# A quad's shared rows fetched and turned first, its last two experts' rows later, and an earlier normalisation on ScalarE in the router stage

## What is computed

```python
x = x + 0.5 * L0_ffn(layernorm(x))          # quantised 256x256 weight plus a low-rank term
x = x + L0_attn(layernorm(x))               # 16 heads, sums over dyadic sets of keys
x = x + 0.5 * L0_ffn(layernorm(x))
x = x + 0.5 * L1_ffn(layernorm(x))          # router, 32 experts, 16 adapters
x = x + L1_attn(layernorm(x))               # linear attention
x = x + 0.5 * L1_ffn(layernorm(x))
...
# L1_ffn: the router takes each normalised row with five of its statistics
ri = concat([xf, stats(xf)]); h = gelu(ri @ r1_w.T + r1_b); probs = softmax(h @ r2_w.T)
topp, topi = top_k(probs, 2)
idx = argsort(-where(routed, probs, -inf), axis=0)[:cap].T     # cap = 160 rows of each expert
up = einsum('eci,eji->ecj', xf[idx], w_up); gate, upv = split(up)
ye = einsum('ecj,eoj->eco', silu(gate) * upv, w_down)
out = zeros.at[idx].add(w * ye)                                # plus the adapters' part
```

## Time and profile before

| | us |
|---|---|
| median of 3 runs | 1788.64 (1785.24 to 1790.99) |
| the profiled execution, device time | 1788.87 |
| its span | 1787.2 |
| TensorE matmul busy | 1488.8 (83% of the span) |
| VectorE busy | 977.1 (55%) |
| ScalarE busy | 728.9 (41%) |
| GpSimd (POOL) busy | 564.3 (32%) |
| mean granted TensorE clock | 0.908 of full speed |

### The profile page before, as it was taken

One profiled execution on the slowest core, in us unless ns is written; L12 is line 12 of the kernel. 1 busy time (PEld: TensorE's weight loads), 2 busy tenths in 40 slices (PEclk: granted clock), 3 DMA queues, 4 the chain that ended last, 5 costly groups with the idle time before them and its releaser, 6 DMA issues. The chain is left out here.

```text
span 1787.2 us, 27066 instructions
## 1 busy us (share of the span) xinstructions
PE 1488.8 (83%) x9512; PEld 1127.3 (63%) x9512; DVE 977.1 (55%) x2816; ACT 728.9 (41%) x1775; POOL 564.3 (32%) x467
## 2 busy tenths in 40 slices
PE   6899989999999678339999997489995459999994
PEld 5566544555554454229889997255553349899994
DVE  8865677787873597855531111356566855521110
ACT  5222147666667375415423232114333425322331
POOL 6522210000000442321636455221211231636535
PEclk9989889999999898559999999699997569999997
DMA  3034363333300022325969894401112326879974
GB/s 104 18 127 129 107 131 63 79 55 79 55 26 1 12 95 83 150 44 174 246 194 258 245 246 65 133 25 35 48 36 95 118 71 201 225 221 247 265 193 47
DMA packets 113493, 212.11 MB, mean 119 GB/s; under 512 B 20085, under 2 KB 79386, under 8 KB 104154
## 3 DMA queue, kind: packets, MB, share of 16 engines
q1 hardware_dynamic: 87066, 178.93, 31.8%
q0 software_dynamic: 26304, 31.60, 11.4%
HBM read 158.71 MB, written 51.38 MB: 118 GB/s over the span
## 5 line engine op out<-in xcount | busy, mean ns | idle before, releaser
L952 DVE TENSOR_REDUCE attnm_top<-psum 128x1 f32<-128x384 f32 (+3 forms) x384 | 212.8, 597 | 56.4 <-PE psum L1037 52.3
L1174 ACT ACTIVATE attnm_prob<-psum 128x512 f32<-128x512 f32 (+1 forms) x384 | 192.1, 530 | 87.6 <-PE psum L1047 81.0
L2328 POOL DMA_INDIRECT x_sum<-moe1e_y,moe_scatter_i x76 | 119.7, 1575 | 128.2 <-ACT moe1e_y L2462 71.0
L2507 DVE SCALAR_TENSOR_TENSOR moe1e_h<-moe1e_gate,psum 128x160 f32<-128x160 f32 x160 | 50.6, 321 | 199.4 <-ACT moe1e_gate L2436 199.1
L2328 POOL DMA_INDIRECT out<-moe2e_y,moe_scatter_i x76 | 119.2, 1568 | 127.7 <-ACT moe2e_y L2462 70.5
L2507 DVE SCALAR_TENSOR_TENSOR moe2e_h<-moe2e_gate,psum 128x160 f32<-128x160 f32 x160 | 50.4, 321 | 198.8 <-ACT moe2e_gate L2436 198.6
L2383 PE MATMUL psum<-moe1e_xgT,moe_w_up 128*128 128x160 f32 x1024 | 152.2, 304 | 2.4 <-ACT moe1e_xgT L2452 2.4
L2383 PE MATMUL psum<-moe2e_xgT,moe_w_up 128*128 128x160 f32 x1024 | 150.7, 302 | 2.4 <-ACT moe2e_xgT L2452 2.4
L2383 PEld LDWEIGHTS psum<-moe1e_xgT,moe_w_up 128*128 128x128 f32 x1024 | 144.2, 193 | 4.8 <-issue 4.8
L2383 PEld LDWEIGHTS psum<-moe2e_xgT,moe_w_up 128*128 128x128 f32 x1024 | 142.7, 192 | 4.8 <-issue 4.8
L1348 POOL DMA_INDIRECT moe_xg<-xn_rows,moe_gather_i x80 | 84.3, 1054 | 159.3 <-DVE moe_gather_i L1536 93.0
(11 more groups left out here) (414 smaller groups left out, 3230.5 us busy)
## 6 DMA issues: line engine op xcount, KB each, us to landing
moe_w_up<-in_expert_up SPq DMA_DIRECT2D x64, 1024.0 KB, 7.5
moe_w_down<-in_expert_down SPq DMA_DIRECT2D x64, 512.0 KB, 3.5
attnm_q_hat<-q_parts SPq DMA_DIRECT2D x72, 128.0 KB, 4.4
moe_a_up<-in_adapter_up SPq DMA_DIRECT2D x32, 256.0 KB, 4.2
q_parts<-attnf_q_part SPq DMA_DIRECT2D x12, 512.0 KB, 2.8
attnm_k_hat<-k_parts SPq DMA_DIRECT2D x72, 64.0 KB, 2.3
x_res<-in_x SPq DMA_DIRECT2D x8, 512.0 KB, 9.4
v_tails<-attnf_v_tail SPq DMA_DIRECT2D x4, 1024.0 KB, 4.3
```

The lines of the kernel that those rows point to most:

```text
L952: nc.vector.tensor_reduce(top[:, n // QUADS % 2, tiles[0]:tiles[-1] + 1, hh:hh + 1], s.ps[:, u.bank, 0:len(tiles) * width].rearrange("p (t ...
L1174: nc.scalar.activation(prob[:, i % NPROB, at:GROUP], s.ps[:, u.bank, at:GROUP], ACT.Exp).then_inc(taken[u.bank], 1)
L2328: nc.gpsimd.indirect_dma_start(total, bass.IndirectOffsetOnAxis(ap=rows, axis=0), y[:, q, k, :], None, bounds_check=TOKENS + SPARE - 1, oo ...
L2507: nc.vector.scalar_tensor_tensor(out=h[:, n % 2, i, :], in0=gate[:, i, :], scalar=1.0 if i < INTER // P else SCALE_A, in1=s.ps[:, u.bank, ...
```

## The change

A second table, `FETCHED`, replaces `TWO` for gathering and turning: tile 4 alone, then tiles 0 and 1, then 2 and 3. The batches of x become separate entries of `ORDER`. For the even quad of a turn, the batch of tiles 2 and 3 is turned and copied after `up` of the first expert, and `up` waits for it only at the third expert of the quad. The odd quad still turns its three batches together. `weights` follows the last batch. In `ffn_router`, `norm(i + 3)` moves from ahead of the gelu to right behind `copy(i + 2)`.

```diff
--- before.py
+++ after.py
@@ -1214,6 +1214,7 @@
 LOW = [4 ** k for k in range(7, -1, -1)]
 ROUNDS = len(HIGH) + len(LOW)
 TWO = [(0, 1), (2, 3), (4,)]
+FETCHED = [(4,), (0, 1), (2, 3)]
 ALONE = TWO[0]
 SIDE, HOTS = 4, 8
 
@@ -1342,7 +1343,7 @@
 
     def gather(self, pool, quad):
         q = quad % 2
-        for i, tiles in enumerate(TWO):
+        for i, tiles in enumerate(FETCHED):
             for k in tiles:
                 at = quad * ST_TILES + k
                 pool.indirect_dma_start(self.xg[:, q, k, :], None, self.rows,
@@ -2035,6 +2036,8 @@
                     r.take(act, i - 4)
                 if 0 <= i + 2 < GROUPS:
                     copy(i + 2)
+                if 0 <= i + 3 < GROUPS:
+                    norm(i + 3)
                 if 0 <= i - 1 < GROUPS:
                     r.absolute(act, i - 1)
                     r.under(act, i - 1)
@@ -2043,8 +2046,6 @@
                     r.copy_s(act, i - 2)
                 if 0 <= i - 1 < GROUPS:
                     r.copy_x(act, i - 1)
-                if 0 <= i + 3 < GROUPS:
-                    norm(i + 3)
                 if 0 <= i - 2 < GROUPS:
                     r.gelu(act, i - 2)
     st.close()
@@ -2223,9 +2224,9 @@
     ORDER = []
     for n in range(2 * EQ):
         if n == 0:
-            ORDER += [("x", 0, None)] + [("up", 0, i) for i in range(PAIRS)]
+            ORDER += [("x", 0, 0), ("x", 0, 1)] + [("up", 0, i) for i in range(PAIRS)] + [("x", 0, 2)]
         if n == 1:
-            ORDER += [("x", 1, None)]
+            ORDER += [("x", 1, j) for j in range(len(FETCHED))]
         if n + 1 < 2 * EQ:
             for i in range(PAIRS):
                 ORDER += [("up", n + 1, i)]
@@ -2243,9 +2244,8 @@
         elif what == "down":
             u_down[n] = banks.use(5)
         else:
-            for j in range(len(TWO)) if what == "x" else (i,):
-                (u_x if what == "x" else u_y)[n, j] = banks.use(6 + ring % 2)
-                ring += 1
+            (u_x if what == "x" else u_y)[n, i] = banks.use(6 + ring % 2)
+            ring += 1
 
     late = m.choices[1]
     STEPS = [("halves", None), ("counts", 0)]
@@ -2343,16 +2343,15 @@
             pool.wait_ge(y_out[q], 16 * (ST_TILES * 2 * TURNS - q * len(ALONE)))
 
     def tensor(pe):
-        def turn_x(t, q):
-            for i, tiles in enumerate(TWO):
-                u = u_x[q, i]
-                pe.wait_ge(x_in[q][i], 16 * len(tiles) * t + 16 * len(tiles))
-                pe.wait_ge(taken[u.bank], u.before(t))
-                for k, tile in enumerate(tiles):
-                    for c in range(CC):
-                        at = (c * len(tiles) + k) * P
-                        ins = nc.tensor.transpose(s.ps[:, u.bank, at:at + P], xg[:, q, tile, c * P:(c + 1) * P], s.ident[:])
-                ins.then_inc(full[u.bank], 1)
+        def turn_x(t, q, i):
+            u, tiles = u_x[q, i], FETCHED[i]
+            pe.wait_ge(x_in[q][i], 16 * len(tiles) * t + 16 * len(tiles))
+            pe.wait_ge(taken[u.bank], u.before(t))
+            for k, tile in enumerate(tiles):
+                for c in range(CC):
+                    at = (c * len(tiles) + k) * P
+                    ins = nc.tensor.transpose(s.ps[:, u.bank, at:at + P], xg[:, q, tile, c * P:(c + 1) * P], s.ident[:])
+            ins.then_inc(full[u.bank], 1)
 
         def turn_y(t, q, i):
             u, last = u_y[q, i], u_down[q * EQ + (TWO[i][-1] if i == 0 else EQ - 1)]
@@ -2369,8 +2368,8 @@
             if i == 0:
                 pe.wait_ge(up_in[k], 32 * t + 16 * q + 16)
                 pe.wait_ge(a_in[k // 2], 64 * t + 32 * q + 32)
-                if k == 0:
-                    for j in range(len(TWO)):
+                for j, tiles in enumerate(FETCHED):
+                    if k == tiles[0] % EQ:
                         pe.wait_ge(taken[u_x[q, j].bank], u_x[q, j].after(t))
             u = u_up[n, i]
             pe.wait_ge(taken[u.bank], u.before(t))
@@ -2414,7 +2413,7 @@
         def run(t, order):
             for what, n, i in order:
                 if what == "x":
-                    turn_x(t, n)
+                    turn_x(t, n, i)
                 elif what == "y":
                     turn_y(t, n, i)
                 elif what == "up":
@@ -2443,14 +2442,14 @@
             nc.scalar.copy(yT[:, q, :, k * P:(k + 1) * P], out_T[:, :, 0:P])
             nc.scalar.copy(yT[:, q, :, tail:tail + CAP - P], out_T[:, :, P:CAP]).then_inc(taken[u.bank], 1)
 
-        def copy_x(t, q):
-            for i, tiles in enumerate(TWO):
-                u, k = u_x[q, i], len(tiles)
-                act.wait_ge(full[u.bank], u.after(t))
-                slots = xgT[:, q].rearrange("p c (k n) -> p c k n", n=CAP)
-                slots = slots[:, :, tiles[0]:tiles[0] + k, 0:P] if tiles[0] < EQ else slots[:, :, :, P:CAP]
-                nc.scalar.copy(slots, s.ps[:, u.bank, 0:CC * k * P].rearrange(
-                    "p (c k n) -> p c k n", c=CC, n=P if tiles[0] < EQ else CAP - P)).then_inc(taken[u.bank], 1)
+        def copy_x(t, q, i):
+            u, tiles = u_x[q, i], FETCHED[i]
+            k = len(tiles)
+            act.wait_ge(full[u.bank], u.after(t))
+            slots = xgT[:, q].rearrange("p c (k n) -> p c k n", n=CAP)
+            slots = slots[:, :, tiles[0]:tiles[0] + k, 0:P] if tiles[0] < EQ else slots[:, :, :, P:CAP]
+            nc.scalar.copy(slots, s.ps[:, u.bank, 0:CC * k * P].rearrange(
+                "p (c k n) -> p c k n", c=CC, n=P if tiles[0] < EQ else CAP - P)).then_inc(taken[u.bank], 1)
 
         def weigh_y(t, q, i):
             u = u_y[q, i]
@@ -2478,7 +2477,7 @@
                 elif what == "down":
                     copy_down(t, n)
                 elif what == "x":
-                    copy_x(t, n)
+                    copy_x(t, n, i)
                 elif what == "y":
                     weigh_y(t, n, i)
                 else:
@@ -2532,7 +2531,7 @@
 
         def run(t, order):
             for what, n, i in order:
-                if what == "x":
+                if what == "x" and i == len(FETCHED) - 1:
                     weights(t, n)
                 elif what == "up":
                     product(t, n, i)
```

## The result

| | before | after |
|---|---|---|
| median of the runs, us | 1788.64 (1785.24 to 1791.51, 11 runs) | 1795.65 (1792.63 to 1800.18, 11 runs) |
| ratio to before | | 1.0039, 95% interval 1.0028 to 1.0050 |
| span of the profiled execution, us | 1787.2 | 1793.9 |
| router stage, first turn to first scores, us | 121.25 | 130.37 |
| first gather to `up`, first / second MoE, us | 10.81 / 10.36 | 8.30 / 8.17 |

The change costs 7.0 us (5.0 to 8.9 by the interval), where 0.4 us less than before was forecast. In its code the lines of the router front and of the MoE's front are one higher than before, those of the experts one lower (L1818, L1826, L1617 stand for L1817, L1825, L1616; L2382, L2353 for L2383, L2354).

A forecast was written before the change was run, and what follows sets the result against it. TensorE was taken to bound the experts' stretch and a loop through several engines the router stage. From 1788.87 us, -4.4 (experts' start), 0 (turn boundaries) and +3.7 (router stage) gave 1788.2 us, range 1783.5 to 1792.6.

The forecast's parts named there:

- the first term: Start of the experts in both MoEs: `up` waits for three gathers instead of five, together -4.4 us.
- The start of the experts, -4.4: `up` starts 2.36 us earlier in the first MoE and 2.01 in the second; bounds -6.2 to -2.5.
- The turn boundaries, 0 with 0.6 to each side: Later quads of each MoE: small gains at even quads and losses at odd ones cancel, 0 us.
- The router stage without the clock, +0.83: Router loop: early group 4 wins 2.08 us, two rounds of 12.72 us lose 2.91; net +0.83 at group 7's turn.
- the rival of the early turn kept: Router stage: TensorE's 5.84 us wait vanishes whole and rounds stay at 10.65 us; 1778.7 us, chance 0.10.
- the one of VectorE: Router stage: VectorE sets the pace, and its normalisations, freed from POOL's bias, save 8.2 us; 1776.3 us, chance 0.04.
- The clock, +2.9 for two of three losses at 1.45: Router stage: longer waits before hidden of groups 0 to 2 drop TensorE's clock, 1.45 us per loss; with +0.83, +3.7.
- The first pause: TensorE's wait before hidden of group 0, one of three taken to grow from 0.96 to 3.03 us.
- the clock stays low: Router stage: the lost clock stays at 1.2 GHz through logits and turn, 3.25 us per round; 1795.1 us, chance 0.07.

The follow-up runs named there:

- x only: The kernel before with only the new order of gathers and expert rows, norm at its old place; 1784.86 us, ratio 0.999.
- Norm only: The kernel before with only norm moved behind the copy, gathers unchanged; 1796.07 us, ratio 1.0047.
- filled kernel: The change plus transposes that nothing reads in TensorE's pauses ahead of group 0's statistics and hidden 1 and 2, router stage alone; 1783.88 us, ratio 0.9968.
- absolute values thrice: The kernel before with two more unused absolute values on ScalarE for each of groups 1, 2 and 3 in the router stage; 1800.38 us, ratio 1.0074.
- boundary filler: The kernel before with the new gather and row order, plus six unread transposes ahead of tile 4's turn and six ahead of `up` at each even quad; 1778.85 us, 0.9955.

## Why the prediction was wrong

The forecast was 1788.2 us and no difference that can be told; measured were 1795.65 us and 7.0 us more. In the profiles the first term came out at -4.7 us where -4.4 was forecast, and the router stage at +9.1 where +3.7 was. The two MoE stages behind their starts add 5.9 us (-0.4 and +1.0 of it in the first passes), where nothing was forecast, and stages that the change does not touch took 3.6 us less.

**The start of the experts, -4.4: right in place, too good in sum.** Both starts gained what the sum gave (2.51 and 2.19 us against 2.36 and 2.01), and from a gather's issue to its first transpose 3.38 to 3.67 us passed, not the 2.3 us worked out from the Trainium skill's page DMA: Bandwidth & Descriptors, section on the anatomy of one DMA. Alone the part measured -1.8 us by the ratio, with an interval from -4.5 to +0.7. The profile of x only loses 1.6 us again behind the second start, of which 1.0 are first passes at the lower clock. A loss of that kind lay in the bounds given.

**The turn boundaries, 0 with 0.6 to each side: the bound was wrong.** The waits and transposes came as worked out. That a boundary can lose the clock was not in the sum. In the change's profile it cost 0.5 us in one MoE and 3.9 in the other, in two other kernels 4.4 and 4.5 us in one MoE. The term should have had an upper end of some 4.5 us for a MoE. Whether the new order brings these losses is not shown. Norm only, in the old order, loses 8.4 us with none in its profile, so they are not the main part of the 7.0.

**The router stage without the clock, +0.83: right.** The filled kernel is the test. From turn 2 to hidden 0 it won 2.07 us (forecast 2.08). From turn 5 to turn 7 it lost 2.35 us (forecast 2.91), for a round of 12.45 instead of 12.72 us. Net that is +0.28 us. The loop copy, norm, absolute, under, count, hidden, turn is the mechanism, and the rival of the early turn kept falls with it, as does the one of VectorE: its normalisations all fell to 1.38 us, and the stage did not get shorter.

**The clock, +2.9 for two of three losses at 1.45: the step that failed.** The place and the cause were right, the size was not. Against the filled kernel the change lost 1.05 us between turn 2 and hidden 0, 0.48 up to turn 5 and 4.64 up to turn 7: 6.2 us for the term that was put at 2.9, with 5.3 as its upper end. Norm only lost the same 6.2 us (1.16, 1.56 and 3.46), divided otherwise. Three things went wrong in the price.

All three pauses lost the clock in norm only, at 1.52 to 1.58 us each in hidden alone. The first pause was misread: TensorE waited 0.29 us ahead of hidden 0, not 0.96, and what grows is the wait ahead of the statistics, to 3.91 us behind the early turn of group 4. The clock lost there delayed hidden 0 by 1 us more. And the slow stretch can outlast hidden. That cost the change 3.66 us in the round of its second loss (16.11 instead of 12.45) and 0.98 in the next, not 1.45. It lost the clock at two pauses of three, as the sum had it, but by luck: behind the long round TensorE waits only 1.04 us ahead of hidden 2, which no step of the forecast held.

The outlasting stretch was the rival "the clock stays low" (1795.1 us, chance 0.07), against which I put that "hidden alone gives TensorE work to bring the clock back". In norm only it did, in the change it did not at group 1: the clock stood at 0.50 from 654.10 to 667.00, while TensorE was busy 12.82 of 12.90 us. That the rival's 1795.1 us is close to the result is luck: of the three pauses one had its long loss in this profile, and the sum was made up by the first pause, hidden of group 6 and the boundaries.

The remaining 2.7 of the stage's 9.1 us lie where the change edits nothing, 1.13 ahead of turn 2 and 1.54 behind turn 7. They are the clock too, but not behind the new pauses, and norm only shows little of either with the same code there (11.00 and 59.51 us).

**Chances.** The upper ends of the terms together gave 1793.1 us, and the result lies above that as well as above the range. I cut the range to 1792.6 and gave 0.07 to slower, although the term with the widest bounds was priced from one row of a pause of 2.93 us that lost the clock for certain. That evidence pointed to three losses of three.

## What to carry to other kernels

Work moved ahead in an engine's order is free only if no loop between engines runs through the new place: here 2 us of ScalarE work made two rounds 2.4 us longer together (12.45 and 12.43 us against 11.88 and 10.65), and that was the smaller part. Price every TensorE pause that grows to 3 us with the work behind it at the lower clock, for each of them, and let the range reach to a slow stretch that outlasts the first matmuls. And before a pause is shortened by reordering, try filling it with work that nothing reads: it recovered 6.2 us in the stretches that it filled, with the order of the change unaltered, but it cost time in a stage where TensorE was busy, and gained nothing where the next engine was late.

## What the runs showed of the hardware

- No length of pause decides alone whether TensorE's clock falls. The pauses of 2.8 to 3.9 us around hidden 0 to 2 lost it every time, two in the change and three in norm only, and one of 2.15 us did with the absolute values thrice (3.24 us for hidden). The one of 3.58 us ahead of hidden 6 lost it before (3.40 us for hidden) and in the change (3.75 us), and kept it with the absolute values thrice and with the boundary filler (1.96 and 1.95 us). At the turn boundaries it was lost at times with no pause over 0.88 us, and kept at others in the same code.
- The slow stretch has no fixed length either. Behind a pause of 2.87 us it ended with hidden (norm only: 3.47 us, logits then 1.08), behind one of 2.84 us it lasted 12.9 us, with TensorE at work nearly throughout.
- The Trainium skill, page TensorE: Matmul & The Clock Gate, part on the clock gate, says that the low clock is the default and that activity releases it. The runs agree with conditions: 27 and 10 transposes in the gaps ahead of `up` did (passes of 4.58 us), 10 alone did not (6.98 us), and six directly ahead of it, with no gap left, nearly did in one MoE (4.93 us) and partly in the other (5.55 us).
- Filler is not free where TensorE is busy: with 60 transposes in the linear attention's router its stretch took 286.5 us, 6.3 more than in the change.
